# Attention bias loaded as one 1 MB transfer per block of four heads, and masked two heads at a time, on one Trainium2 core

## The chip, the cores and the metric

The kernel runs on 1 core of a Trainium2 chip, as one program. The metric is the time of one execution on the device in microseconds (us); lower is better. Engines are named as in the profile: PE is the matrix engine, DVE the vector engine, ACT the scalar engine, POOL the GpSimd engine, SP the engine that only issues transfers here.

## What is computed

Two layers on x of shape (8, 512, 512), float32. The first is a feed-forward layer (or, by a condition per sample, a small 4-wire circuit), then a layer norm. The second is a transformer layer with 16 heads of 32 columns, modulated by a time step embedding. Its attention reads a bias of 8 x 16 x 512 x 512 float32, 128 MB in all, and a mask of 8 x 1 x 512 x 512 bytes:

```
q, k, v = x @ Wq + bq, x @ Wk + bk, x @ Wv + bv            # 16 heads of 32
scores = einsum('bhqd,bhkd->bhqk', q / sqrt(32), k) + attention_bias
scores = where(src_mask, -inf, scores)
probs = softmax(scores)
ctx = einsum('bhqk,bhkd->bhqd', probs, v)
x = x + ctx @ Wo + bo
x = x + gelu2(layernorm(x) * g2 + beta2 @ W1 + b1) @ W2 + b2   # the feed-forward part, in words
```

## The kernel before

Three stages follow one another, with a barrier between them: `ffn_stage` (first layer), `attention_stage`, and `ffn_stage` again. Only the attention stage is touched.

**Work units.** A sample b (8 of them, `each_pair` unrolls odd and even ones) has 16 blocks m. A block is a group of four heads (`m // 4`) and 128 queries (`m % 4`); each of its four heads is one unit j: a 128x512 tile of scores. Blocks are counted 0 to 127 over all samples below where the text gives a global number.

**Order of the work.** Each engine has a list of its own, written out by hand, and they meet through semaphores. For block m, PE makes the scores of block m+1 (line 1247), the product with v of block m-1 (line 1264, the context), then four times: turns unit j of block m (line 1276, four 128x128 transposes of the exponentials into PSUM) and does three or so matmuls of another product beside it (line 1197). DVE adds scores and bias and finds the row's top in one instruction (line 1100, which waits for `masked` and `score_mm`), copies the turned units 1 and 3 out of PSUM (line 1107), and ACT takes the exponential (line 982) and copies the units 0 and 2 (line 989). PE's context of block m waits for those copies (`pt_even`, `pt_odd`), and PE's turn of unit j+2 waits for the copy of unit j.

Once per four blocks DVE has more to do. In a block with m % 4 == 3 it takes the reciprocals (line 1115); in one with m % 4 == 0 it normalises the group before (line 1120, `normalize`) and writes the low half of the context (line 1124, `context_lo`, which reads `at_normal` and `at_cth`, both in SBUF) between its scores of unit 3 and its copy of unit 3. In blocks 11 to 14 of a sample it also turns one quarter of the next sample's byte mask into bfloat16 after the copy of unit 3 (line 1079, `set_mask`). After blocks 8 and 9 PE turns the next sample's x (line 1204, `turn_x`), which waits for both copies.

**The bias.** `bias` holds 16 tiles of 128x512 (four blocks). SP loads two heads at a time (line 906, 512 KB), into the slots of block m as soon as PE has turned the first two, and then the last two, units of block m: these are the data of block m+4. POOL adds the mask, one head per instruction (line 951, bias += mask, in place), and counts `masked`; `set_mask` waits for that count before it overwrites a quarter of the mask. After the masks of block 13 POOL adds the output bias to the residual (line 955, four instructions). SP also issues, between the bias loads, the next x (line 917, at m = 0), the next mask (line 920, m = 1), the store of x2 (line 923, m = 4) and the residual (line 927, m = 8).

## Time and profile before

| | us |
|---|---|
| median of 3 runs | 2644.94 (2638.65 to 2649.93) |
| the profiled execution's own time | 2651.21 |
| its span | 2649.4 |
| PE busy over the span | 2447.0 (92%) |
| DVE busy | 1404.1 (53%) |
| ACT busy | 993.1 (37%) |
| POOL busy | 979.5 (37%) |
| attention stage, scores of the first block to the end of the last | about 893 to 1875 |

The profile is of one execution. Busy time is summed per engine; PE counts the matrix engine's pipelined matmuls, so its 92% is not 92% of its peak. The idle time of an engine is put down to whatever released it, from the semaphore events. DMA columns give the busy share of the 16 transfer engines: about half in the attention stage.

### The profile page before, as it was taken

Reading aid. Unit: us, or ns where it says so; the run is one execution under the profiler, and the core shown is the slowest. Engines: PE = TensorE matmul, PEld = TensorE weight load, DVE = VectorE, ACT = ScalarE, POOL = GpSimd, SP = SyncE. Lnnn points to the kernel's source line nnn. Section 1 sums busy time; section 2 is a strip of 40 time slices with the busy share of each in tenths; the row PEclk is TensorE's granted clock in tenths of the full one; section 3 lists DMA queues with packets and bytes.
Section 4 is the critical chain, followed back from the end, with each engine's and each line's share of the span. In section 5 each row is a group of like instructions: output and inputs, shape, how many; then the busy total and the mean of one; then the engine's idle time right before and its main releaser. Section 6 shows DMA issues by size and latency. Waiting matters only on the chain. (4 is left out here: it accounts for less than half of the span.)

```text
span 2649.4 us, 44273 instructions
## 1 busy us (share of the span) xinstructions
PE 2447.0 (92%) x16100; PEld 1920.0 (72%) x16100; DVE 1404.1 (53%) x2668; ACT 993.1 (37%) x1977; POOL 979.5 (37%) x806
## 2 busy tenths in 40 slices
PE   5999999999995789898989999998489999999999
PEld 4687787787783567676766667676378888888887
DVE  5354454454454677777677777777453333333322
ACT  4232231232230566666566656566231212111211
POOL 0031332332240565656565657666020122012200
PEclk9999999999997899999999999999789999999999
DMA  5201110110111555454555555545331001100100
GB/s 161 72 33 40 40 38 33 40 53 18 40 40 55 195 158 174 153 179 153 165 166 181 152 164 168 161 144 165 92 111 48 32 16 47 47 23 25 47 32 16
DMA packets 133361, 243.69 MB, mean 92 GB/s; under 512 B 13212, under 2 KB 17452, under 8 KB 133184
## 3 DMA queue, kind: packets, MB, share of 16 engines
q1 hardware_dynamic: 133184, 241.39, 28.4%
q8 instruction: 103, 1.69, 0.3%
q14 instruction: 74, 0.61, 0.1%
HBM read 216.17 MB, written 25.20 MB: 91 GB/s over the span
## 5 line engine op out<-in xcount | busy, mean ns | idle before, releaser
L951 POOL TENSOR_TENSOR at_bias<-at_bias,at_mask 128x512 f32<-128x512 f32 x512 | 587.3, 1173 | 381.0 <-DMA at_bias<-in_fside_Bx16xSxS 343.3
L648 DVE CAST L_hh<-L_hid 128x512 fp32r<-128x512 f32 x256 | 122.5, 478 | 797.9 <-PE L_acc L746 758.4
L487 ACT ACTIVATE L_hid<-L_turn,L_b1c 128x512 f32<-128x512 f32 x256 | 176.5, 690 | 983.9 <-PE L_turn L285 978.8
L283 PE MATMUL L_turn<-L_xth,L_w1h 128*128 128x512 f32 x1024 | 406.7, 397 | 7.7 <-ACT L_hid L487 5.4
L744 PE MATMUL L_acc<-L_w2h,L_hh 128*128 128x512 f32 x1024 | 403.1, 394 | 8.6 <-DVE L_hl L650 8.6
L284 PE MATMUL L_turn<-L_xth,L_w1l 128*128 128x512 f32 x1024 | 400.7, 391 | 0.0
L285 PE MATMUL L_turn<-L_xtl,L_w1h 128*128 128x512 f32 x1024 | 400.2, 391 | 0.0
L746 PE MATMUL L_acc<-L_w2l,L_hh 128*128 128x512 f32 x1024 | 400.1, 391 | 0.0
L745 PE MATMUL L_acc<-L_w2h,L_hl 128*128 128x512 f32 x1024 | 400.0, 391 | 0.0
L982 ACT ACTIVATE at_bias<-at_bias,at_neg_top 128x512 f32<-128x512 f32 x512 | 363.5, 714 | 44.3 <-DVE at_neg_top L1100 44.1
L1100 DVE CUSTOM_DVE_ANT_0 at_bias<-at_score,at_bias 128x512 f32<-128x512 f32 x512 | 333.0, 684 | 55.9 <-issue 29.8
L1276 PE MATMUL at_turn<-ident,at_bias 128*128 128x128 f32 x2048 | 314.7, 280 | 47.6 <-DVE at_pt L1107 33.7
L1276 PEld LDWEIGHTS at_turn<-ident,at_bias 128*128 128x128 f32 x2048 | 241.1, 142 | 131.1 <-issue 78.0
L989 ACT ACTIVATE at_pt<-at_turn 128x512 f32<-128x512 f32 x256 | 152.8, 597 | 285.4 <-PE at_turn L1276 285.3
L283 PEld LDWEIGHTS L_turn<-L_xth,L_w1h 128*128 128x128 f32 x1024 | 193.5, 189 | 74.5 <-issue 31.6
L650 DVE TENSOR_TENSOR L_hl<-L_hid,L_hh 128x512 fp32r<-128x512 f32 x256 | 231.8, 905 | 8.8
L744 PEld LDWEIGHTS L_acc<-L_w2h,L_hh 128*128 128x128 f32 x1024 | 193.2, 189 | 49.5 <-DVE L_hl L650 6.1
L1107 DVE COPY at_pt<-at_turn 128x512 f32<-128x512 f32 x256 | 174.2, 681 | 98.1 <-PE at_turn L1276 98.0
L285 PEld LDWEIGHTS L_turn<-L_xtl,L_w1h 128*128 128x128 f32 x1024 | 193.3, 189 | 41.3
L746 PEld LDWEIGHTS L_acc<-L_w2l,L_hh 128*128 128x128 f32 x1024 | 193.1, 189 | 40.6
L745 PEld LDWEIGHTS L_acc<-L_w2h,L_hl 128*128 128x128 f32 x1024 | 193.4, 189 | 39.3
L284 PEld LDWEIGHTS L_turn<-L_xth,L_w1l 128*128 128x128 f32 x1024 | 193.6, 189 | 38.7
(201 smaller groups left out, 3116.0 us busy)
## 6 DMA issues: line engine op xcount, KB each, us to landing
at_bias<-in_fside_Bx16xSxS SPq DMA_DIRECT2D x256, 512.0 KB, 3.7
L_xin<-in_x SPq DMA_DIRECT2D x8, 1024.0 KB, 5.4
L_xres<-in_x SPq DMA_DIRECT2D x8, 1024.0 KB, 5.4
at_xin<-x_scratch SPq DMA_DIRECT2D x8, 1024.0 KB, 6.5
at_xres<-x_scratch SPq DMA_DIRECT2D x8, 1024.0 KB, 6.9
L_xin<-x_scratch SPq DMA_DIRECT2D x8, 1024.0 KB, 5.5
L_xres<-x_scratch SPq DMA_DIRECT2D x8, 1024.0 KB, 5.5
x_scratch<-L_xres SPq DMA_DIRECT2D x7, 1024.0 KB, 4.3
```

What stands on the lines that cost most here:

```text
L283: nc_mm = pe.matmul(out, ah, bh, start=i == 0, stop=False)
L284: nc_mm = pe.matmul(out, al, bh, start=False, stop=False)
L285: nc_mm = pe.matmul(out, ah, bl, start=False, stop=i == n - 1)
L487: nc.scalar.activation(hid[m % 2][:, :], turn[m % 2][:, :], func, bias=b1c[:, m:m + 1]).then_inc(h_act, 1)
L650: nc.vector.tensor_tensor(hl[m % 2][:, :], hid[m % 2][:, :], hh[m % 2][:, :].bitcast(F32), ALU.subtract)\
L744: pe.matmul(acc[i][:, :], hh[m % 2][:, cut], w2h[:, m, :], start=m == 0, stop=False)
L745: pe.matmul(acc[i][:, :], hl[m % 2][:, cut], w2h[:, m, :], start=False, stop=False)
L746: mm = pe.matmul(acc[i][:, :], hh[m % 2][:, cut], w2l[:, m, :], start=False, stop=m == FT - 1)
L951: nc.gpsimd.tensor_tensor(tile, tile, mask[:, m % TT, :], ALU.add).then_inc(masked, 1)
L982: nc.scalar.activation(tile, tile, ACT.Exp, bias=neg_top[:, n % SLOTS:n % SLOTS + 1], scale=-1.0, accum_out=sums[:, n:n + 1]).then_inc(exp ...
L1100: nc.vector.tensor_tensor_reduce(bias[:, slot, :], score[j][:, :], bias[:, slot, :], -1.0, -MASKED, ALU.add, ALU.min, neg_top[:, slot:slot ...
L1276: mm = pe.transpose(turn[n % 2][:, k * P:(k + 1) * P], bias[:, n % SLOTS, k * P:(k + 1) * P], keep.ident[:, :])
```

## The change

Three things, all in the attention stage:

1. The bias of a block of four heads is one transfer of 1 MB in place of two of 512 KB, with one semaphore per ring position in place of two.
2. SP issues it when unit 3 of block m is turned. Before, the first half was issued when unit 1 was turned.
3. POOL's mask addition covers two heads (128x1024, the mask read twice by a zero stride) in one instruction, which adds 2 to `masked`.

```
-        bias_in = [[sem(f"bias_in{r}{i}") for i in range(2)] for r in range(4)]
+        bias_in = [sem(f"bias_in{r}") for r in range(4)]
...
-            def load_bias(b, m, i):
+            def load_bias(b, m):
                 tile, u = divmod(m, TT)
-                h = GROUP * tile + 2 * i
-                src = t["fside_Bx16xSxS_0"][b, h:h + 2, u * P:(u + 1) * P, :].rearrange("h p n -> p h n")
-                sp.dma_start(bias[:, m % 4 * 4 + 2 * i:m % 4 * 4 + 2 * i + 2, :], src).then_inc(bias_in[m % 4][i], 16)
+                src = t["fside_Bx16xSxS_0"][b, GROUP * tile:GROUP * tile + GROUP, u * P:(u + 1) * P, :].rearrange("h p n -> p h n")
+                sp.dma_start(bias[:, m % 4 * 4:m % 4 * 4 + 4, :], src).then_inc(bias_in[m % 4], 16)
...
-                        for i in range(2):
-                            wait_apart(sp, passed_sp, (turned, b * UNITS + GROUP * m + 2 * i + 2))
-                            load_bias(b + (m + 4) // BLOCKS, (m + 4) % BLOCKS, i)
+                        wait_apart(sp, passed_sp, (turned, b * UNITS + GROUP * m + GROUP))
+                        load_bias(b + (m + 4) // BLOCKS, (m + 4) % BLOCKS)
...
-                    for j in range(GROUP):
-                        if j % 2 == 0:
-                            pool.wait_ge(bias_in[m % 4][j // 2], b * 64 + 16 * (m // 4 + 1))
-                        tile = bias[:, m % 4 * 4 + j, :]
-                        nc.gpsimd.tensor_tensor(tile, tile, mask[:, m % TT, :], ALU.add).then_inc(masked, 1)
+                    pool.wait_ge(bias_in[m % 4], b * 64 + 16 * (m // 4 + 1))
+                    for i in range(GROUP // 2):
+                        tiles = bias[:, m % 4 * 4 + 2 * i:m % 4 * 4 + 2 * i + 2, :]
+                        nc.gpsimd.tensor_tensor(tiles, tiles, mask[:, m % TT:m % TT + 1, :].to_broadcast([P, 2, S]), ALU.add)\
+                            .then_inc(masked, 2)
```

The order of instructions on PE, DVE and ACT is the same as before. On SP it changes as follows, here around block 8 of a sample, where the residual is loaded. `at_turned` is PE's count of turned units; a register instruction stands before each wait. Before:

```order
L906 ISA [waits at_turned]
L906 DMA at_bias<-in_fside_Bx16xSxS 128x2x512
L71 REGISTER_ALU
L906 ISA [waits at_turned]
L906 DMA at_bias<-in_fside_Bx16xSxS 128x2x512
L71 REGISTER_ALU
L927 ISA [waits at_stored]
L927 DMA at_xres<-x_scratch 128x4x512
L71 REGISTER_ALU
L906 ISA [waits at_turned]
L906 DMA at_bias<-in_fside_Bx16xSxS 128x2x512
```

and now:

```order
L905 ISA [waits at_turned]
L905 DMA at_bias<-in_fside_Bx16xSxS 128x4x512
L71 REGISTER_ALU
L925 ISA [waits at_stored]
L925 DMA at_xres<-x_scratch 128x4x512
L71 REGISTER_ALU
L905 ISA [waits at_turned]
L905 DMA at_bias<-in_fside_Bx16xSxS 128x4x512
```

One wait and one transfer of four heads stand where two of each stood; the residual's load keeps its place between blocks.

On POOL, the masks of block 13 of a sample, the four additions to the residual and the masks of block 14. `at_bias_in..` is the semaphore of a bias load. Before:

```order
L951 TENSOR_TENSOR at_bias<-at_bias,at_mask 128x512 [waits at_bias_in10]
L951 TENSOR_TENSOR at_bias<-at_bias,at_mask 128x512
L951 TENSOR_TENSOR at_bias<-at_bias,at_mask 128x512 [waits at_bias_in11]
L951 TENSOR_TENSOR at_bias<-at_bias,at_mask 128x512
L955 TENSOR_TENSOR at_xres<-at_xres,at_bor 128x512 [waits at_xres_in]
L955 TENSOR_TENSOR at_xres<-at_xres,at_bor 128x512 x3
L951 TENSOR_TENSOR at_bias<-at_bias,at_mask 128x512 [waits at_bias_in20]
```

and now:

```order
L947 TENSOR_TENSOR at_bias<-at_bias,at_mask 128x1024 [waits at_bias_in1]
L947 TENSOR_TENSOR at_bias<-at_bias,at_mask 128x1024
L952 TENSOR_TENSOR at_xres<-at_xres,at_bor 128x512 [waits at_xres_in]
L952 TENSOR_TENSOR at_xres<-at_xres,at_bor 128x512 x3
L947 TENSOR_TENSOR at_bias<-at_bias,at_mask 128x1024 [waits at_bias_in2]
L947 TENSOR_TENSOR at_bias<-at_bias,at_mask 128x1024
```

A block has one wait and two instructions of 128x1024 where it had two waits and four instructions of 128x512; there is no wait between the two any more.

## Rows read from the trace of the kernel before

**Rows 1.** Windows view, the attention stage: stretch; us; busy of PE, PEld, DVE, ACT, POOL; PEclk; DMA; GB/s
```profile
900.00:1875.00 975.00, 886.88 (x9302) 673.63 (x9301) 719.28 (x1510) 608.53 (x1449) 606.60 (x529) 0.96 0.51 160
```

**Rows 2.** Waits view, 1000 to 1850: us in total, times, longest us
```profile
POOL at_bias L951 <- DMA at_bias<-in_fside_Bx16xSxS: 309.8, 159, 6.4
...
PE at_turn L1276 <- DVE at_pt L1107: 26.8, 28, 2.4
...
PE at_turn L1204 <- DVE at_pt L1107: 18.9, 12, 2.0
...
DVE at_bias L1100 <- POOL at_bias L951: 3.3, 7, 0.8
```

**Rows 3.** Groups of instructions on POOL, 860 to 1900
```profile
L951 POOL TENSOR_TENSOR at_bias<-at_bias,at_mask 128x512 f32<-128x512 f32 x512 | 587.3, 1173 | 381.0 <-DMA at_bias<-in_fside_Bx16xSxS 343.3 <-DVE at_mask L1079 36.1
L955 POOL TENSOR_TENSOR at_xres<-at_xres,at_bor 128x512 f32<-128x512 f32 x32 | 40.1, 1289 | 0.0
```

**Rows 4.** DMA view: issues, KB each, median us from issue to landing
```profile
at_bias<-in_fside_Bx16xSxS SPq DMA_DIRECT2D x256, 512.0 KB, 3.7
L_xin<-in_x SPq DMA_DIRECT2D x8, 1024.0 KB, 5.4
...
at_xres<-x_scratch SPq DMA_DIRECT2D x8, 1024.0 KB, 6.9
```

**Rows 5.** Timeline, block 124: its first mask, and DVE's first use of it
```profile
1826.86 1.16 POOL L951 TENSOR_TENSOR at_bias<-at_bias,at_mask 128x512 f32<-128x512 f32 x1 [3.06 <-DMA at_bias<-in_fside_Bx16xSxS]
...
1835.85 0.69 DVE L1100 CUSTOM_DVE_ANT_0 at_bias<-at_score,at_bias 128x512 f32<-128x512 f32 x1 [0.65 <-issue]
```

**Rows 6.** DVE lines by themselves: count, min/median/max ns, first and last start
```profile
L650 DVE TENSOR_TENSOR L_hl<-L_hid,L_hh x256: 691/693/1677, 33.5 to 2639.3; 128x512 fp32r<-128x512 f32 x128
...
L1079 DVE TENSOR_SCALAR at_mask<-at_mask x32: 414/417/1527, 879.3 to 1748.4; 128x512 bf16<-128x512 uint8 x32
...
L1124 DVE SCALAR_TENSOR_TENSOR at_ctl<-at_normal,at_bvc,at_cth x32: 744/748/3078, 928.7 to 1873.8; 128x512 fp32r<-128x512 f32 x32
```

**Rows 7.** Timeline, 1848 to 1852: POOL's masks of block 127 and DVE beside them
```profile
1849.19 2.29 POOL L951 TENSOR_TENSOR at_bias<-at_bias,at_mask 128x512 f32<-128x512 f32 x2
...
1848.95 3.08 DVE L1124 SCALAR_TENSOR_TENSOR at_ctl<-at_normal,at_bvc,at_cth 128x512 fp32r<-128x512 f32 x1 [0.30 <-ACT at_cth L1001]
```

**Rows 8.** Timeline of SP: issues of a block's second half
```profile
1134.31 0.37 SPq L906 DMA_DIRECT2D at_bias<-in_fside_Bx16xSxS  x1
...
1196.17 0.37 SPq L906 DMA_DIRECT2D at_bias<-in_fside_Bx16xSxS  x1
...
1212.92 0.37 SPq L906 DMA_DIRECT2D at_bias<-in_fside_Bx16xSxS  x1
...
1229.35 0.38 SPq L906 DMA_DIRECT2D at_bias<-in_fside_Bx16xSxS  x1
```

**Rows 9.** Timeline of DVE in blocks 32, 40, 43 and 44
```profile
1140.74 0.75 DVE L1124 SCALAR_TENSOR_TENSOR at_ctl<-at_normal,at_bvc,at_cth 128x512 fp32r<-128x512 f32 x1
...
1202.69 0.75 DVE L1124 SCALAR_TENSOR_TENSOR at_ctl<-at_normal,at_bvc,at_cth 128x512 fp32r<-128x512 f32 x1
...
1230.04 0.61 DVE L1079 TENSOR_SCALAR at_mask<-at_mask 128x512 bf16<-128x512 uint8 x1
1231.55 0.75 DVE L1088 SCALAR_TENSOR_TENSOR at_nat<-at_gen,at_bqc,at_nat 128x512 fp32r<-128x512 f32 x1 [0.91 <-ACT at_nat L972]
...
1235.85 0.75 DVE L1124 SCALAR_TENSOR_TENSOR at_ctl<-at_normal,at_bvc,at_cth 128x512 fp32r<-128x512 f32 x1
1236.52 0.68 DVE L1107 COPY at_pt<-at_turn 128x512 f32<-128x512 f32 x1
```

**Rows 10.** Timeline of PE: after block 40, and the context of block 44
```profile
1204.30 1.96 PE L1204 MATMUL at_turn<-ident,at_xin 128*128 128x128 f32 x8 [1.96 <-DVE at_pt L1107]
...
1237.61 0.64 PE L1264 MATMUL at_ctx<-at_pt,at_v 128*32 128x128 f32 x16
```

**Rows 11.** Timeline of POOL: the last two masks of block 43
```profile
1199.63 2.27 POOL L951 TENSOR_TENSOR at_bias<-at_bias,at_mask 128x512 f32<-128x512 f32 x2 [1.51 <-DMA at_bias<-in_fside_Bx16xSxS]
```

More of the change, by code:

```diff
@@ L899, in _ @@
             sp.dma_start(mask8[:, :, :], rows(t["mask_Bx1xSxS_bk0"][0, 0])).then_inc(mask_in, 16)
-            def load_bias(b, m, i):
+            def load_bias(b, m):
                 tile, u = divmod(m, TT)
-                h = GROUP * tile + 2 * i
-                src = t["fside_Bx16xSxS_0"][b, h:h + 2, u * P:(u + 1) * P, :].rearrange("h p n -> p h n")
-                sp.dma_start(bias[:, m % 4 * 4 + 2 * i:m % 4 * 4 + 2 * i + 2, :], src).then_inc(bias_in[m % 4][i], 16)
+                src = t["fside_Bx16xSxS_0"][b, GROUP * tile:GROUP * tile + GROUP, u * P:(u + 1) * P, :].rearrange("h p n -> p h n")
+                sp.dma_start(bias[:, m % 4 * 4:m % 4 * 4 + 4, :], src).then_inc(bias_in[m % 4], 16)
             for m in range(4):
                 sp.wait_ge(w_lo, m + 1)
-                for i in range(2):
-                    load_bias(0, m, i)
+                load_bias(0, m)
             def body(b, odd, first, last):
@@ L928, in body @@
                     if m + 4 < BLOCKS or not last:
-                        for i in range(2):
-                            wait_apart(sp, passed_sp, (turned, b * UNITS + GROUP * m + 2 * i + 2))
-                            load_bias(b + (m + 4) // BLOCKS, (m + 4) % BLOCKS, i)
+                        wait_apart(sp, passed_sp, (turned, b * UNITS + GROUP * m + GROUP))
+                        load_bias(b + (m + 4) // BLOCKS, (m + 4) % BLOCKS)
             each_pair(sp, body)
```

## Prediction

> **What bounds the kernel now.** I read the stretch of the attention stage first, then its waits, then the timeline around the few instructions in which DVE and POOL meet. The stretch says that PE bounds the stage: 887 of 975 us busy, DVE 719, POOL 607, the transfer engines 51% [rows 1]. The waits say who holds PE in what is left: mostly DVE's copy of a turned unit (line 1107), 26.8 us in front of the next turn and 18.9 us in front of the turn of x [rows 2]. POOL's idle time is nearly all waiting for the bias, 309.8 us, and DVE waits for POOL for 3.3 us in all [rows 2]. So the masks are made well ahead. The tightest place is in the last sample: block 124's first mask starts at 1826.86 and DVE takes that tile at 1835.85, 9.0 us later [rows 5]; in the other 127 blocks that lead is longer.
>
> **The change, part by part.** I sum against the profiled execution (span 2649.4, own time 2651.2) and add the sum to the median, 2644.9, which lies 6 us below it.
>
> *Fewer transfers.* 128 issues of 0.37 us [rows 8] leave SP, on which nothing waits but transfers; the bytes and the 2 KB pieces are the same. 0 us, hidden behind the 9 us lead above.
>
> *Later masks.* A block's first two heads are now asked for with the last two, 2.3 to 3.8 us later, and 1 MB lands 5.4 us after its issue when it is alone on the queue, against 3.7 for 512 KB; behind other traffic it took 6.9 [rows 4]. The first `masked` count comes after two heads, not one, 1.1 us more. Together 2.3 to 3.8, plus 1.7 to 3.2, plus 1.1: 5.1 to 8.1 us of a lead that is 9.0 less the first mask's 1.16 at the tightest place, 7.8 us. That takes both of the longest values at once, and there the issue is the short one; it holds: 0 us. Were the lead gone, DVE's line 1100 would wait, and ACT's exponential and PE's turn behind it.
>
> *Two heads per instruction.* One head takes 1.17 us, of which the trace does not show a fixed part; the pair now takes 2.27 [rows 3, 11]. The bounds for one instruction of 128x1024 are 1.2 us (all of it fixed) and 2.6 (twice line 955's 1289 ns). I take 2.25, what a pair takes, since the instruction still handles 1024 elements. POOL is idle 38% of the stage, so its own time is worth 0 us either way. What matters is what it blocks.
>
> *POOL and DVE in each other's way.* This is the term on which I forecast. Some DVE instructions take far longer than their median beside a POOL instruction: line 650, with both inputs in SBUF, 693 ns mostly but up to 1677; line 1079 417 and up to 1527; line 1124, again two SBUF inputs, 748 in 31 of 32 cases and 3078 once [rows 6]. The extra 984 and 1110 ns fit in the rest of one POOL instruction. In the one long case of line 1124, POOL ran masks without a gap: DVE asked at 1848.95, POOL went from one instruction to the next at 1849.19, and once more before its pair ended at 1851.48, and DVE was done at 1852.03, so that it got in only at about 1851.3 [rows 7]. The Trainium skill (SBUF — State Buffer, "Who interferes with whom") says it in the same way: the read and write ports shared by the two are an exclusive lock, a DVE instruction with two SBUF inputs needs it against a POOL instruction that reads SBUF, and the second to start blocks until the first has finished. The trace agrees for lines 650 and 1079 (one instruction's rest), and not in rows 7, where DVE was passed over twice. By the page the sum below is the forecast's, by rows 7 the first rival's.
>
> Before, line 1124 nearly always falls into a gap of POOL. In block 40 the last masks of block 43 run from 1199.63 to 1201.90 [rows 11] and line 1124 starts at 1202.69 [rows 9]. Now the masks of block 43 start when a transfer issued at 1196.17 [rows 8] has landed, 1196.17 + 5.4 = 1201.6, and run to 1203.8 and 1206.1. Line 1124 asks in the middle of the first. With the lock passed on at the next end it waits 1.1 us. PE is already waiting 1.96 us for DVE's very next instruction, the copy, in front of the turn of x [rows 10], so all of it reaches PE: 1.1 us in each of the 7 samples that turn an x, 8 us.
>
> Block 32 (block 0 of a sample): 1134.31 + 5.4 = 1139.7, first mask to 1142.0, line 1124 at 1140.74 [rows 8, 9]: it waits 1.2 us. Here PE has room: in block 44, built alike, the copy ends at 1237.20 [rows 9] and PE's context starts at 1237.61 [rows 10], 0.4 us. 0.8 us x 7 = 5 us. In block 4 of a sample line 1124 comes later against its load and meets the second instruction's end, 0.6 us against 0.4: 1 us over the run.
>
> Block 12 of a sample is the worst, because line 1079 comes in front of it. POOL's masks of block 45, asked for at 1212.92 [rows 8], run 1218.3 to 1222.8, line 955 four times to 1227.9, and then the masks of block 46, 1227.9, 1230.1, 1232.4. Line 1079 starts at 1230.04 [rows 9], at the boundary; if it just misses it, it waits 2.2 us. DVE has 0.91 us of idle time behind it [rows 9] and is then busy without a gap, so line 1124 asks 1.3 us later, at 1237.1. The masks of block 47, asked for at 1229.35 [rows 8], run 1234.8, 1237.0, 1239.3: the wait is 2.1 us. DVE's copy is 3.4 us late, PE 3.0. 3.0 x 7 = 21 us. If line 1079 slips in at the boundary, line 1124 waits 1.1 and this is 0.7 x 7 = 5 us. The other calls of line 1079 wait 0.4 to 1 us in front of gaps of DVE that cover it: 0.
>
> Sum: 8 + 5 + 1 + 21 = 35 us, and PE, which bounds the stage, has nothing with which to make it good. 2644.9 + 35 = **2680 us**, 1.3% slower. What a measurement of this kernel can tell from no change is about 0.5%, 13 us.
>
> **The rivals.**
>
> *The lock is held to the end of POOL's run.* Rows 7 speak for it, and line 1124 is the very instruction; the 56 long cases of line 650 speak against, none over one instruction. There is no wait between a block's two instructions now, so a run is 4.5 us. Blocks 8: to 1206.1, 3.4 x 7 = 24; block 0: 3.0 x 7 = 21; block 12: 21; 1 more: 67 us, 2712.
>
> *No meeting, so not slower.* The margin is small: line 1124 asks 6.5 us after the issue. If 1 MB of bias lands after 6.5 us or more, as the residual's does with its 6.9 [rows 4], line 1124 of blocks 0, 8 and 12 gets in before POOL starts and POOL waits instead, which costs nothing. Much the same follows if the two-head instruction takes not 2.25 but the 1.2 us of its lower bound, since line 1124 would then ask 0.1 us before the first one's end. Then only a few waits of line 1079 are left, 0 to 8 us: 2645 to 2653, taken as 2648. Against it: the 5.4 us of a lone 1 MB load.
>
> *Faster.* All the waiting at the shared ports that the stage has now is 2.3 us at line 1124 and some 4 us at line 1079. If short instructions removed it, and the change had no meeting elsewhere, 2638. That is still within what can't be told from no change. More would need PE to wait less for copies, and nothing in the change shortens DVE's own chain.
>
> *The lead is used up.* If each 1 MB took 6.9 us behind the residual and the sample's last blocks lost their lead, line 1100 would wait in the last sample, some 1 us in four blocks: 2649. It is small and adds to any case.
>
> **How the numbers follow.** The forecast, meeting with the lock passed on at an instruction's end: 0.42, its own range 19 us (line 1079 slips in) to 45 us (a two-head instruction of 2.6 us). Held to the run's end: 0.22. No meeting, or the lead alone: 0.32. Faster or the remainder: 0.04. 0.03 of the forecast's chance lies within 13 us of before. So faster 0.03, within 0.5% 0.35, slower 0.62. The range must reach to both neighbours: from 2643 to 2713.
>
> **What would show it.** In the profile after, line 1124 should have a median of about 1.8 us in place of 0.75, and longest values near 2.9; under the rival near 4.1. Line 1079 should be long in block 11 only. The wait of PE's turn of x for line 1107 should grow from 18.9 us by about 8, and waits of the context (line 1264) for line 1107 should appear. POOL's instruction should be 2.25 us, and the load land 5.4 us after its issue. The prediction is wrong if line 1124 stays at 0.75 us, or if DVE waits for POOL at line 1100 for more than a few us.

## The result, and the profile after

The changed kernel takes 2656.64 us, median of 6 runs (2654.53 to 2659.48), beside 2646.16 for the kernel before on the same chip: a ratio of 1.0043 with an interval of 1.0026 to 1.0059, 10.5 us slower. The forecast was 35 us slower, 1.3%. The direction came out, at less than a third of its size, and inside the half per cent of "no change" but for the interval's upper end. The two profiled executions that are read below took 2657.24 and 2651.21 us, so they differ by 6.0 us and not by 10.5.

I read the views of after in the order of [rows 1 to 6]. First the windows view of the attention stage (columns as in [rows 1]):

```profile
900.00:1875.00 975.00, 885.21 (x9263) 671.73 (x9262) 746.74 (x1507) 607.12 (x1449) 578.73 (x281) 0.96 0.47 160
```

DVE is busy 27 us longer with the same work, 746.7 against 719.3 [rows 1]. POOL is busy 28 us less, with half as many instructions. The waits view, 1000 to 1850:

```profile
POOL at_bias L947 <- DMA at_bias<-in_fside_Bx16xSxS: 345.9, 103, 8.4
...
PE at_turn L1273 <- DVE at_pt L1104: 29.1, 28, 2.4
...
PE at_turn L1201 <- DVE at_pt L1104: 21.0, 12, 2.5
```

PE's turn of x waits 2.1 us more for DVE's copy than in [rows 2], where the forecast wanted 8, and the turn of a unit 2.3 us more. The 3.3 us that DVE's scores waited for POOL are gone from the view. The masks, their load, and the two DVE lines that meet them (groups of POOL, DMA view, and the lines by themselves):

```profile
L947 POOL TENSOR_TENSOR at_bias<-at_bias,at_mask 128x1024 f32<-128x1024 f32 x256 | 558.0, 2202 | 418.5 <-DMA at_bias<-in_fside_Bx16xSxS 382.3
```

```profile
at_bias<-in_fside_Bx16xSxS SPq DMA_DIRECT2D x128, 1024.0 KB, 5.0
```

```profile
L1121 DVE SCALAR_TENSOR_TENSOR at_ctl<-at_normal,at_bvc,at_cth x32: 744/1099/1953, 927.0 to 1879.7; 128x512 fp32r<-128x512 f32 x32
...
L1076 DVE TENSOR_SCALAR at_mask<-at_mask x32: 416/1442/2398, 880.6 to 1754.2; 128x512 bf16<-128x512 uint8 x32
```

So the meeting takes place. (In these lines the three numbers behind the count are the shortest, the median and the longest duration in ns.) The median of `context_lo` (line 1121, 1124 before) grew from 748 to 1099 ns, not to the 1800 forecast. `set_mask` (line 1076, 1079 before) grew from 417 to 1442. Above those old medians, the 32 calls of `context_lo` wait 10.6 us in sum (2.3 before), and the 28 of `set_mask` that lie inside the samples 24.3 (2.2 before): 30 us of new waiting, for an end that is 10.5 us later.

**Block 40, the place of the forecast's first term.** Timeline of SP, POOL, DVE and PE:

```profile
1195.12 0.37 SPq L905 DMA_DIRECT2D at_bias<-in_fside_Bx16xSxS  x1
...
1199.93 2.13 POOL L947 TENSOR_TENSOR at_bias<-at_bias,at_mask 128x1024 f32<-128x1024 f32 x1 [2.17 <-DMA at_bias<-in_fside_Bx16xSxS]
...
1202.03 2.57 POOL L947 TENSOR_TENSOR at_bias<-at_bias,at_mask 128x1024 f32<-128x1024 f32 x1
...
1201.64 0.98 DVE L1121 SCALAR_TENSOR_TENSOR at_ctl<-at_normal,at_bvc,at_cth 128x512 fp32r<-128x512 f32 x1
...
1203.47 1.97 PE L1201 MATMUL at_turn<-ident,at_xin 128*128 128x128 f32 x8 [2.18 <-DVE at_pt L1104]
```

DVE asks 6.5 us after the issue, as forecast. But the load was there after 4.8 us (1199.93 - 1195.12), not 5.4; POOL's first instruction took 2.13, not 2.25; and DVE was done at 1202.62, so that it was in at about 1202.62 - 0.75 = 1201.87 if it then took the 0.75 us that it takes alone, 0.19 before the end that the trace gives for POOL's first instruction, 1202.06. Together 0.9 us, so the wait is 0.23 us and not 1.1. All of it reaches PE, whose wait is 2.18 where it was 1.96 [rows 10]. The mechanism is the one forecast, and its place on the clock was missed by less than a microsecond.

**Block 44, the place of the 21 us.** Timeline of DVE and POOL:

```profile
1228.07 2.13 POOL L947 TENSOR_TENSOR at_bias<-at_bias,at_mask 128x1024 f32<-128x1024 f32 x1
...
1228.90 1.59 DVE L1076 TENSOR_SCALAR at_mask<-at_mask 128x512 bf16<-128x512 uint8 x1
1230.41 0.75 DVE L1085 SCALAR_TENSOR_TENSOR at_nat<-at_gen,at_bqc,at_nat 128x512 fp32r<-128x512 f32 x1
...
1233.32 2.16 POOL L947 TENSOR_TENSOR at_bias<-at_bias,at_mask 128x1024 f32<-128x1024 f32 x1 [3.12 <-DMA at_bias<-in_fside_Bx16xSxS]
...
1234.72 1.30 DVE L1121 SCALAR_TENSOR_TENSOR at_ctl<-at_normal,at_bvc,at_cth 128x512 fp32r<-128x512 f32 x1
```

`set_mask` came 0.83 us after a boundary of POOL's run, not just behind it, and waited 1.17 us. The next DVE instruction, which had 0.91 us of idle time in front of it [rows 9], now has none. The whole trace stands 1.1 us earlier than that of before here, and 1234.72 is 1.13 earlier than the 1235.85 of [rows 9]: `context_lo` asks no later than it did. It waits 0.55 us, of which PE's slack of 0.4 takes most.

**The start of sample 3 (samples counted from 0), which the forecast did not name.** Timeline of DVE and PE, then the windows view around it (columns as in [rows 1], the last but two the granted clock):

```profile
1248.99 2.40 DVE L1076 TENSOR_SCALAR at_mask<-at_mask 128x512 bf16<-128x512 uint8 x1
...
1252.53 3.34 DVE L1112 RECIPROCAL at_normal<-at_sums 128x512 f32<-128x512 f32 x1
...
1256.56 0.77 PE L1273 MATMUL at_turn<-ident,at_bias 128*128 128x128 f32 x4 [2.08 <-DVE at_pt L1104]
1256.98 0.78 PE L1194 MATMUL at_gen<-at_wvh,at_xth 128*128 128x512 f32 x1
```

```profile
1256.50:1258.30 1.80, 1.74 (x7) 1.49 (x8) 1.73 (x5) 1.25 (x3) 1.37 (x1) 0.61 0.11 18
1258.30:1261.70 3.40, 1.20 (x9) 0.69 (x7) 0.00 (x0) 0.39 (x3) 0.00 (x0) 0.50 0.83 275
1261.70:1264.00 2.30, 2.30 (x28) 1.52 (x32) 0.53 (x1) 0.96 (x2) 0.18 (x1) 0.50 1.00 344
1264.00:1268.00 4.00, 4.00 (x37) 3.20 (x30) 1.51 (x6) 1.65 (x4) 4.00 (x2) 0.61 0.29 105
```

The same place in the trace of before, PE's timeline and the windows:

```profile
1256.27 0.63 PE L1276 MATMUL at_turn<-ident,at_bias 128*128 128x128 f32 x4 [0.90 <-DVE at_pt L1107]
1256.65 0.48 PE L1197 MATMUL at_gen<-at_wvh,at_xth 128*128 128x512 f32 x1
```

```profile
1256.20:1258.30 2.10, 1.76 (x11) 1.37 (x11) 1.74 (x5) 1.52 (x4) 0.61 (x1) 1.00 0.28 80
...
1261.70:1264.00 2.30, 2.30 (x37) 1.91 (x29) 1.91 (x5) 0.93 (x2) 1.76 (x2) 0.52 0.13 29
1264.00:1268.00 4.00, 4.00 (x24) 3.34 (x23) 2.06 (x7) 3.56 (x8) 0.00 (x0) 0.85 0.77 289
```

This `set_mask` asked at 1248.99, just behind a boundary of POOL's run, and waited 1.98 us, the "just misses" of the forecast, in another block. Behind it stands DVE's long reciprocal, so the copy behind that is late and PE idles 2.08 us in place of 0.90: 1.2 of the 1.98 us reach PE, 0.8 are covered. Right behind that idle time the granted clock is at 0.61 and 0.50 (the level of 1.2 GHz), where in the trace of before it is still at 1.00, and a matmul of 512 columns takes 0.78 in place of 0.48 us. The clock falls here in before too, but later and for less time: 5 us on, behind 2.60 us in which PE waits for nothing that the profile shows ("issue"). The last two lines of each window view show it, 0.52 and 0.85 against 0.50 and 0.61 at the same times in after. The period that ends with the first turn of sample 3 is 2.8 us longer than before, that of sample 5, built alike, 2.4. Not all of this can be put down to `set_mask`: at these two places every trace has that second idle time of PE, from 2.0 to 3.9 us, and in e3 and e8 below, where no `set_mask` waits there, the same periods come out up to 1.5 and 2.4 us longer than in before. A clean case is the start of sample 1 in a second trace of the changed kernel (e11): `set_mask` waits 1.93 us, PE idles 2.03 in place of 0.90, its clock is at 0.50 from 1013.0 to 1016.4, and the period is 10.80 in place of 8.10 us. Of these 2.7 us, 1.1 are idle time and the rest comes with the clock.

Over the stage the two traces differ as follows. A period is the time from one block's first turn of a unit to the next block's; each figure is the sum over the samples of what the changed kernel's period is longer, for the period that ends with the block named, in us. The second pair are two further traces of the same two kernels (e11 and e12, profiled executions of 2656.24 and 2644.83 us), and e7 is an experiment below.

| period ending with | first pair | second pair | e7 against before |
|---|---|---|---|
| block 0 (start of a sample) | +5.2 | +3.3 | +3.3 |
| block 1 | +0.2 | +0.4 | +2.6 |
| block 5 | +0.3 | 0.0 | +3.2 |
| blocks 9 and 10 | +3.7 | +5.3 | +7.8 |
| blocks 13 and 14 | -1.9 | +4.0 | +6.7 |
| others | -0.2 | -2.2 | -0.1 |
| block 4 of the first sample to block 127 | +7.3 | +10.8 | +23.6 |

The -1.9 is the last sample's: the 3.08 us of line 1124 in [rows 7] lies there in before, whose period is 2.6 us longer than that of after. Without the last sample blocks 13 and 14 give +1.1 us in the first pair and +1.2 in the second. The last sample also adds 2.0 to the +3.7 of blocks 9 and 10, with PE at the lower clock there in after alone and no x to turn.

**Block 8 at the same clock.** Blocks 9 and 10 swing most from pair to pair because of the clock. In block 8 PE's idle time in front of the turn of x is 1.96 us in six of the seven samples that turn one, in before as in e12, and around it the granted clock falls, not always and not for equally long. Windows of PE alone, block 8 of samples 5, 1 and 2 in e12, which is the kernel before, then of sample 2 in before and in after (us; busy of PE; PEclk; DMA; GB/s):

```profile
1571.91:1580.25 8.34, 5.31 (x72) 1.00 0.75 265
1074.34:1084.21 9.87, 6.84 (x72) 0.83 0.67 220
1195.92:1206.67 10.75, 7.72 (x72) 0.70 0.58 198
```

```profile
1198.88:1209.64 10.76, 7.73 (x73) 0.73 0.58 199
```

```profile
1197.84:1208.81 10.97, 7.72 (x73) 0.70 0.69 242
```

The same block of the same kernel takes 8.34, 9.87 or 10.75 us with the mean clock at 1.00, 0.83 or 0.70. In before and in after the clock was at the lower level for equally long in all seven samples, so these two can be compared: after's period is longer by 0.38, 0.43, 0.22, 0.25, 0.35, 0.53 and 0.29 us, and its `context_lo` waits 0.37, 0.44, 0.23, 0.27, 0.34, 0.54 and 0.28. The wait reaches the end whole, 2.5 us over the run. In e8, where `context_lo` does not wait, the six samples with the same clock agree with before within 0.01 us.

Could the clock be the cause of the 10.5 us? Over the executions on record the mean granted clock is 0.969 in the changed kernel and 0.969 in the kernel before. Among the 69 executions of the kernel before whose clock is on record, the time falls as the clock rises (correlation -0.82, 1.7 us for each 0.001). By that slope, the difference between the two kernels' clocks, 0.0005, is worth an estimated 0.8 us. So the clock blurs the single traces, and it is not what makes the loss.

### The profile page after: what moved, and what is told of

It is laid out like the page before. It is cut to its first block and busy times, and to the rows that moved or that the text cites. A ratio compares the mean times of both kernels' runs of the same rounds, so it can differ in the third digit from the quotient of the medians.

```text
span 2655.4 us, 43580 instructions
## 1 busy us (share of the span) xinstructions
PE 2450.7 (92%) x16100; PEld 1922.3 (72%) x16100; DVE 1435.3 (54%) x2668; ACT 992.4 (37%) x1977; POOL 950.0 (36%) x550
## 5 line engine op out<-in xcount | busy, mean ns | idle before, releaser
L947 POOL TENSOR_TENSOR at_bias<-at_bias,at_mask 128x1024 f32<-128x1024 f32 x256 | 558.0, 2202 | 418.5 <-DMA at_bias<-in_fside_Bx16xSxS 382.3
```

The lines of the kernel that those rows point to most:

```text
L947: nc.gpsimd.tensor_tensor(tiles, tiles, mask[:, m % TT:m % TT + 1, :].to_broadcast([P, 2, S]), ALU.add)\
```

## The experiments

The theories that the runs were to tell apart: that the *place* of the masks makes the cost, because of the moment of the load (the forecast's, with its size corrected); that the *length* of POOL's instruction does, or the 1 MB *transfer*, or the lost *lead*. Ratios are against the kernel before (2646.6 to 2647.4 us in these sessions), with their intervals.

### One half of the change at a time

e1 keeps the 1 MB load and masks one head at a time:

```
-                    for i in range(GROUP // 2):
-                        tiles = bias[:, m % 4 * 4 + 2 * i:m % 4 * 4 + 2 * i + 2, :]
...
+                    for j in range(GROUP):
+                        tile = bias[:, m % 4 * 4 + j, :]
+                        nc.gpsimd.tensor_tensor(tile, tile, mask[:, m % TT, :], ALU.add).then_inc(masked, 1)
```

> The changed kernel with one mask instruction per head (1.17 us each) in place of one per two heads; the 1 MB load, begun when the whole block is turned, stays. Ports theory (the cost is DVE waiting for POOL at the shared ports, and it comes from the masks' later place, not from the length of an instruction): masks start 5.0 us after the issue, so that DVE's context_lo, 6.5 us after it, still meets a run of masks; its median is 1.1 to 1.8 us against 0.75 before, set_mask is long too but by at most 1.2 us a time; the time is 3 to 9 us above before. Length theory (only the two-head instruction makes waits that reach PE): same as before within 3 us. Transfer theory (the cost is the load itself): the whole 10 us stay.

e2 keeps the loads of before and masks two heads at a time, each pair behind its own wait:

```
+                    for i in range(GROUP // 2):
+                        pool.wait_ge(bias_in[m % 4][i], b * 64 + 16 * (m // 4 + 1))
+                        tiles = bias[:, m % 4 * 4 + 2 * i:m % 4 * 4 + 2 * i + 2, :]
+                        nc.gpsimd.tensor_tensor(tiles, tiles, mask[:, m % TT:m % TT + 1, :].to_broadcast([P, 2, S]), ALU.add)\
+                            .then_inc(masked, 2)
```

> The kernel before with only the masks changed: two heads in one instruction, each pair after its own 512 KB load. Ports theory: POOL's runs stand where they stood, context_lo still falls into gaps and stays at 0.75 us; set_mask of block 11 of a sample waits up to 2.1 us in place of 1.1, which DVE's idle time covers: 0 to 3 us above before. Length theory: most of the 10 us. Transfer theory: no difference from before.

Measured: e1 2658.06 us, 1.0038 (1.0024 to 1.0053), all of the loss; e2 2645.24 us, 0.9991 (0.9981 to 1.0001), none. The two lines by themselves, in e1:

```profile
L1120 DVE SCALAR_TENSOR_TENSOR at_ctl<-at_normal,at_bvc,at_cth x32: 745/1051/4103, 929.0 to 1879.4; 128x512 fp32r<-128x512 f32 x32
...
L1075 DVE TENSOR_SCALAR at_mask<-at_mask x32: 416/778/2053, 879.7 to 1752.9; 128x512 bf16<-128x512 uint8 x32
```

and in e2:

```profile
L1124 DVE SCALAR_TENSOR_TENSOR at_ctl<-at_normal,at_bvc,at_cth x32: 740/747/1334, 930.2 to 1865.9; 128x512 fp32r<-128x512 f32 x32
...
L1079 DVE TENSOR_SCALAR at_mask<-at_mask x32: 409/416/2361, 880.8 to 1743.6; 128x512 bf16<-128x512 uint8 x32
```

With the load late and the instructions short, `context_lo` waits as in after. With the instructions long and the load early it is at 747 ns. The two-head instruction makes `set_mask` wait in block 11 of every sample, to 1.3 to 1.7 us (8.0 us in sum; the 2361 ns are of a call ahead of the first sample), in front of DVE's 0.91 us of idle time, and the kernel is no slower for it. The length theory falls, and with it goes the forecast's fear of line 1079 in block 11. e1 by itself fits the transfer theory as well as the place theory, since all of the loss stays (the place theory had 3 to 9 us, and 10.1 came); the next pair parts them. And the loss does not follow the sum of the waits: `set_mask` waits 11.7 us inside the samples of e1 against 24.3 in after, for the same loss.

### Masks that hardly read

e3 (the changed kernel) and e4 (the kernel before) add the mask to 2 of the 512 columns; POOL keeps its place, its waits and its counts:

```
-                        tiles = bias[:, m % 4 * 4 + 2 * i:m % 4 * 4 + 2 * i + 2, :]
+                        tiles = bias[:, m % 4 * 4 + 2 * i:m % 4 * 4 + 2 * i + 2, 0:2]
```

> The changed kernel with the mask added to 2 of the 512 columns of each head only (the rest of the mask is left out), so that POOL's instructions are very short and hold no port. To be read against the kernel before with the same cut. Ports theory: context_lo at 0.75 and set_mask at 0.42 us throughout, and the two cut kernels are equal within 3 us. Transfer theory: this one is still 7 to 10 us slower than the cut kernel before.

> The kernel before with the mask added to 2 of 512 columns only (the rest of the mask is left out). Both theories: 0 to 5 us under the kernel before, the most that the few port waits and the waits for set_mask are worth there.

Measured: e3 2644.88 us, 0.9991 (0.9982 to 1.0000); e4 2644.40 us, 0.9995 (0.9983 to 1.0007). With POOL nearly idle the changed load costs nothing, with the same 1 MB transfers at the same moments. The transfer theory falls. A lack of lead would vanish too where the masks take no time, so the lead is left to e8. The line of `context_lo` in e3 has no wait left (maximum 753 ns, 1953 in after):

```profile
L1121 DVE SCALAR_TENSOR_TENSOR at_ctl<-at_normal,at_bvc,at_cth x32: 745/748/753, 929.1 to 1869.7; 128x512 fp32r<-128x512 f32 x32
```

e4 shows what the meetings of the kernel before are worth: 1.3 us by its ratio, 4.5 at most, and its interval allows none.

### The masks moved by a microsecond

e7 is the changed kernel with two POOL additions of 160 columns on a tile of their own ahead of each block's masks, 456 ns each, so that the masks begin 0.9 us later:

```
+                    for i in range(2):
+                        nc.gpsimd.tensor_tensor(spare[:, :], bor[:, 0:160], bor[:, 0:160], ALU.add).then_inc(spared, 1)
+                        pool.wait_ge(spared, b * 2 * BLOCKS + 2 * m + i + 1)
```

> The changed kernel with two short POOL additions on a spare tile (160 columns each, chained by a semaphore) ahead of each block's masks, so that a run of masks starts some 0.9 us later after its load. Sizes theory (the prediction's mechanism holds and only the point at which context_lo meets the masks was off: 0.3 us of the first instruction were left, not 1.1): context_lo is now 1.9 to 2.2 us long in blocks 0, 8 and 12 of a sample, the block after 8 grows by another 0.7 to 0.9 us and those after 0 and 12 by 0.5 to 0.8; 10 to 20 us above the changed kernel, about 2670. Absorption theory (DVE's later work takes up any such wait): within 4 us of the changed kernel.

Measured: 2676.66 us, 1.0124 (1.0108 to 1.0141), 20 us above the changed kernel. The line of `context_lo`, and PE's wait in front of the turn of x, 900 to 1875 (20.1 us before, 22.2 after):

```profile
L1124 DVE SCALAR_TENSOR_TENSOR at_ctl<-at_normal,at_bvc,at_cth x32: 745/1986/2384, 930.4 to 1899.1; 128x512 fp32r<-128x512 f32 x32
```

```profile
PE at_turn L1204 <- DVE at_pt L1107: 28.6, 13, 3.6
```

The median wait is 1.24 us now, what the forecast had assumed for the change itself. The loss against before is 30 us by the medians, near the 35 of the forecast, and PE's turn of x waits 8.5 us longer, where it had said 8. The table above shows that the loss lies in the blocks it named, behind blocks 0, 4, 8 and 12, and at the sample starts, which it did not. So the term of block 8 was priced well, wait and way to the end, and only the moment of the meeting was not. The others were not: e7 gives 2.6 us at block 0 (forecast 5), 3.2 at block 4 (1), 6.7 at block 12, or 8.2 without the last sample (21), and 3.3 at the sample starts (0). That the sum comes near 35 is in part luck. The waits of `set_mask` are about as long in sum as in after (27.7 us inside the samples, 24.3 in after); what grew is the sum at `context_lo`, from 10.6 to 31.4.

### The masks moved out of the way

e8 is the changed kernel with POOL held, by semaphores that exist already, until DVE has copied unit 3 and has done the `set_mask` behind it. The masks come later than in the changed kernel, in DVE's other stretches; in block 8 of the first sample they begin 1.5 us after `context_lo` has asked, against 1.6 us before it in after:

```
-                        pool.wait_ge(mask_set, b * TT + m + 1)
+                        pool.wait_ge(mask_set, b * TT + min(m + 3, TT))
+                    elif m >= 14 and not last:
+                        pool.wait_ge(mask_set, b * TT + TT + m - 13)
+                    if not first or m >= 3:
+                        pool.wait_ge(pt_odd, b * (UNITS // 2) + 2 * m - 4)
```

> The changed kernel with POOL's masks of block m+3 held back until DVE has copied unit 3 of block m (behind context_lo) and, in the four blocks concerned, has done set_mask. So the masks are later still, but meet neither. Ports theory: context_lo at 0.75 us and set_mask at 0.42 us but for the odd case, the time is back at that of the kernel before, 2643 to 2650. Lead theory (the masks come too late): slower than the changed kernel, with DVE waiting for masked in front of its scores.

Measured: 2646.65 us, 1.0002 (0.9992 to 1.0013). Later masks, and all of the loss gone. The line of `context_lo`, and what POOL waits for, 900 to 1875:

```profile
L1125 DVE SCALAR_TENSOR_TENSOR at_ctl<-at_normal,at_bvc,at_cth x32: 744/747/752, 929.3 to 1870.8; 128x512 fp32r<-128x512 f32 x32
```

```profile
POOL at_bias L951 <- DVE at_pt L1108: 339.8, 95, 8.1
```

One meeting is left: `set_mask` of block 11 waits 0.92 us in each of the seven samples, for the last of the additions to the residual, and nothing comes of it. POOL has time for the holding back: its waits for the load have become waits for the copy. With the lead shorter than in the changed kernel and no loss, the lead theory falls; DVE's scores wait for POOL nowhere in this view. The loads are those of the changed kernel, the instructions too, and only the place of the masks differs: the place is the cause. How the 10.5 us divide between `context_lo` and `set_mask` no run shows by itself, since e8 moves the masks away from both.

### The moment of the load alone

e10 is the kernel before with nothing merged: both 512 KB loads of a block are issued when unit 3 is turned.

```
+                        wait_apart(sp, passed_sp, (turned, b * UNITS + GROUP * m + GROUP))
                         for i in range(2):
-                            wait_apart(sp, passed_sp, (turned, b * UNITS + GROUP * m + 2 * i + 2))
                             load_bias(b + (m + 4) // BLOCKS, (m + 4) % BLOCKS, i)
```

> The kernel before, with its two loads of 512 KB and one mask instruction per head, but both loads issued when unit 3 is turned. So the moment moves and nothing is merged. Place theory (what counts is where the run of four masks falls against DVE's context_lo, 6.5 us after the issue): the run is from about 3.5 to 8.1 us after the issue, context_lo meets its third instruction and waits 0.2 to 1.1 us, and the time is 5 to 20 us above before. If only the 1 MB transfer counts: same as before.

Measured: 2653.52 us, 1.0020 (1.0011 to 1.0028).

```profile
L1124 DVE SCALAR_TENSOR_TENSOR at_ctl<-at_normal,at_bvc,at_cth x32: 745/1009/4362, 929.9 to 1873.5; 128x512 fp32r<-128x512 f32 x32
```

The moment alone brings the same waits at `context_lo` (11.9 us in sum over all 32, as in e1, of which 3.6 and 3.4 are one call of the last sample) and nearly the same at `set_mask` (12.5 us inside the samples, 11.7 in e1), and a loss of 5.3 us, between 2.9 and 7.4. e1 lost 10.1 (6.4 to 14.0). The moment makes at least a good part of the loss. Where the other half is in e1 and after, the runs leave open: it is neither in the sums of these waits nor in the mean granted clock (0.969 in both), and the intervals of e1 and e10 overlap a little.

### The same two again

> The changed kernel once more, for a second trace. Ports theory: the same waits at context_lo (1.0 to 1.3 us in blocks 8, 12) and set_mask, 2653 to 2660. In the first trace 5.2 of 5.7 us lay at two places, the starts of samples 3 and 5, where a set_mask of block 14 had waited 2 us in front of the long reciprocal and PE ran at half clock for a while. If that is part of the mechanism, it is there again in samples where that set_mask is long; if it was chance, it is elsewhere or nowhere.

> The kernel before once more, for a second trace and as a control of the timing: 2640 to 2652, ratio 1 within 0.15%; context_lo at 0.75 us in all blocks but the odd one in the last sample.

Measured: e11 2657.42 us, 1.0047 (1.0034 to 1.0060); e12 2646.88 us, 1.0002 (0.9993 to 1.0012). The size of the loss repeats; its place does so only in part. In the second pair (table above) the sample starts give less, a late `set_mask` now in front of sample 1, and blocks 9 and 13 more. The traces of the unchanged kernel differ by 7.5 us over the stage between themselves (939.9 and 932.4, first turn of block 4 to that of block 127). Of these, 4.3 lie in the period that ends with block 9, where e12 was at the lower clock for less time, and 2.6 in that of block 13, which has the long call of [rows 7] in before alone: the longest `context_lo` of e12 is 0.95 us. So a difference of one pair of traces says little about a term of one or two microseconds, unless the clock is the same in both.

### A shorter reciprocal

I took DVE's reciprocal, 3.35 us in front of a copy that PE waits for, to be what makes late copies costly. It computes 512 columns of which 16 differ. e5 (changed kernel) and e6 (kernel before) take it of the 16 sums and spread it with a copy:

```
-                of = sums[:, phase * PHASE:(phase + 1) * PHASE].unsqueeze(2).to_broadcast([P, PHASE, HD])
-                nc.vector.reciprocal(spread, of).then_inc(inv_set, 1)
+                nc.vector.reciprocal(inv[:, :], sums[:, phase * PHASE:(phase + 1) * PHASE]).then_inc(inv_small, 1)
+                dve.wait_ge(inv_small, b * PHASES + phase + 1)
+                nc.vector.tensor_copy(spread, inv[:, :].unsqueeze(2).to_broadcast([P, PHASE, HD])).then_inc(inv_set, 1)
```

> The changed kernel with the reciprocals taken on 128x16 and spread to 128x512 by a copy, in place of one reciprocal of 128x512 (3.35 us): DVE is some 2.3 us shorter once per four blocks. PE waits about 34 us in 32 places for the copy behind that instruction; they should go: 20 to 35 us under the changed kernel. Against the same edit of the kernel before: slack theory (port waits cost time only where DVE is late already): equal within 4 us; if they cost wherever they fall: still some 10 us above it.

> The kernel before with the same short reciprocal and copy. 20 to 35 us under the kernel before, by the 34 us that PE waits behind the long reciprocal. If those waits only move to the next copy, less than 5.

Measured: e5 2616.33 us, 0.9897 (0.9881 to 0.9912); e6 **2598.98 us**, 0.9826 (0.9811 to 0.9842), the fastest version here, 47.6 us under the kernel before. Groups of DVE in before, the long one, and in e6:

```profile
L1115 DVE RECIPROCAL at_normal<-at_sums 128x512 f32<-128x512 f32 x32 | 107.1, 3348 | 1.0 <-ACT at_bias L982 1.0
```

```profile
L1117 DVE COPY at_normal<-at_inv 128x512 f32<-128x512 f32 x32 | 27.3, 853 | 1.1
...
L1115 DVE RECIPROCAL at_inv<-at_sums 128x16 f32<-128x16 f32 x32 | 7.9, 248 | 1.0 <-ACT at_bias L983 1.0
```

and PE's waits for the copies in e6, 900 to 1875 (the first was 20.1, the second 33.7 before):

```profile
PE at_turn L1206 <- DVE at_pt L1108: 20.1, 13, 2.0
...
PE at_turn L1278 <- DVE at_pt L1108: 3.8, 6, 0.6
```

DVE has 72 us less to do, and the 33.7 us that PE waited behind the reciprocal are nearly gone. The gain of 47.6 is more than those 30 and more than I expected. The mean granted clock of e6 is 0.973 against 0.969, by the slope given above an estimated 6 to 7 us; the remaining ten or so I did not separate. With this edit the change costs 17.4 us (2616.33 - 2598.98), not 10.5: with the reciprocal's wait gone the waits at the ports do not become cheap. The theory that they would be absorbed once DVE has slack is wrong. Nor is each of them dearer: there are more of them, probably since the shorter DVE work moves `context_lo` against the masks. Its waits sum to 17.5 us in e5 and 1.1 in e6, against 10.6 and 2.3 in after and before, and in block 4 of a sample it waits 0.95 to 1.29 us in six of the eight samples, where in after it waited in two. And some 5 of the 17.4 us go with the clock (0.970 in e5, 0.973 in e6; the same slope, an estimate). PE still waits 20.1 us for the copy behind `context_lo` in front of its turn of x in e6, and in e5 the periods that end with blocks 9 and 10 are 8.4 us longer in sum, more than any others; the median of block 9 over the samples that turn an x is 10.73 us in e5 and 9.68 in e6, in part by the clock again.

e9 puts the guard of e8 into e5:

> The changed kernel with both the short reciprocal and the masks held back behind DVE's copy and set_mask. Ports theory: the 17 us by which the changed kernel with the short reciprocal lies above the old one with the same edit (2616 against 2599) are all port waits, so holding the masks back gives them back: 2596 to 2604. If part of the 17 us comes from the load, 2605 or more.

Measured: 2605.66 us, 0.9848 (0.9835 to 0.9861). The guard gives back 10.7 of the 17.4 us, and the time misses the 2596 to 2604 expected if all 17.4 were port waits that it removes. The expectation laid 2605 or more to the load; of the 6.7 us that stay the timeline shows another source, in block 12 of each sample (POOL and DVE of e9):

```profile
1210.84 5.46 POOL L957 TENSOR_TENSOR at_xres<-at_xres,at_bor 128x512 f32<-128x512 f32 x4
...
1216.26 4.25 POOL L952 TENSOR_TENSOR at_bias<-at_bias,at_mask 128x1024 f32<-128x1024 f32 x2
...
1219.32 1.75 DVE L1127 SCALAR_TENSOR_TENSOR at_ctl<-at_normal,at_bvc,at_cth 128x512 fp32r<-128x512 f32 x1
```

The guard held the masks of block 13 back, the four additions to the residual come behind them, and the masks of block 14 are pushed into `context_lo`, which waits 1.0 us. The guard moved a meeting there instead of removing it, and the periods that end with block 13 are 5.0 us longer in sum than in e6. I did not run a guard for this one, so a share of the load in the rest is not excluded.

## Why the prediction came out as it did

**Fewer transfers, 0 us.** Right as far as the runs tell: e3, with 128 transfers of 1 MB, is at 0.9991.

**Later masks, 0 us of lead.** Right: DVE's scores do not wait for POOL in after, and e8 has later masks still and loses nothing.

**Two heads per instruction, 2.25 us.** The duration was near: 2.13 to 2.15 us where no DVE instruction comes between, and it costs nothing by itself (e2).

**POOL and DVE in each other's way, +35 us. This is the step that failed.** Its mechanism was right, the meeting of POOL's masks with DVE at the ports, passed on at an instruction's end; its size was wrong, above all in the terms of block 12 (21 forecast, 1.1 measured) and block 8 (8 forecast, 2.5 measured), and a term at the sample starts was put at nothing:

- *Block 8, 1.1 us x 7 = 8.* Measured 0.23 us in block 40 and 0.22 to 0.53 over the seven samples, 2.5 us together at the same clock. It rested on three figures that were all a little high: the load at 5.4 (4.8 there, median 5.0), the instruction at 2.25 (2.13), the ports passed on at the instruction's end (some 0.19 earlier). Each is off by 0.1 to 0.6 us; the term is a small difference of larger numbers and shrank to less than a third, in block 40 to a fifth. The 5.4 was taken from a 1 MB load of x in another stage [rows 4].
- *Block 12, 3.0 us x 7 = 21.* Measured +0.16 us a sample. It took a wait of 2.2 us for line 1079, where 1.2 was found, of which DVE's 0.91 us of idle time left next to nothing; and the second meeting of 2.1 us needed the first. The prediction had named the other case (line 1079 slipping in at the boundary, 5 us) and chose the dearer, with no row that spoke for it. This one choice was 16 of the 35 us. The measured case was neither of the two: line 1079 asked 0.83 us behind the boundary.
- *Blocks 0 and 4, 5 + 1.* Measured 0.2 and 0.3. The wait in block 0 is 0.33 to 0.47 us in five samples and none in two, PE's slack there 0.4.
- *Missing:* the `set_mask` of block 14 in front of the long reciprocal: 5.2 us in the first pair at two sample starts, where the size of each is uncertain, and 2.7 at the clean one in the second. The prediction put "the other calls of line 1079" at 0, covered by gaps of DVE. Of the wait of this call only 0.8 us are covered: 1.98 us made PE idle 1.2 us more, 1.93 us 1.1, and 1.10 us in e7 0.3, and behind the two long ones the clock fell as well.

**The rivals.** *Held to the end of POOL's run* (2712): no single wait in after is longer than one instruction (2.40 us with its own 0.42 in it). It is not dead all the same: three calls in other traces waited to the end of a run (last section). *No meeting* (2648): nearer by its time than the forecast (its own range ends at 2653, the forecast's begins at 2664), wrong by its mechanism, since the meetings are there and e3 or e8 take 10 us away with them. *Lead used up* (2649): did not happen. e7 shows that the forecast's mechanism gives nearly the forecast's time when the masks begin 0.9 us later, though with the terms divided otherwise; the measured case lay between the forecast and the rival, on a slope of some 20 us in 0.9 us. A range of cases was right here, and the chance should have been spread over that slope, not put on one end.

**What would show it.** Line 1124 at 1.8 us: 1.10. Line 1079 long in block 11 only: wrong, it is 1.76 us in block 12 as well, and long at times in blocks 13 and 14. The turn of x +8: +2.1. New waits of the context for the copy: none, there is one of 1.2 us in either trace.

## What to carry to other kernels

The loss came from the place of the masks on the clock, and e8 got it back without touching the loads. Moving a load moves the work that waits for it, and that work can meet another engine at a shared port though no wait in the program joins them; before merging transfers, look at what the consumer will then run beside, instruction by instruction. A cost that is the difference of several durations (landing, length, handover) should be given as a range over the slack beside it, since 0.9 us decided here between 10 and 30 us. Before two traces are compared block by block, look whether the granted clock is the same in both: here it alone moved a block from 8.3 to 10.8 us. And if an engine that waits for loads a third of its time can be held until the other one's critical instructions are through, the conflict costs nothing (e8), as long as the held work does not pile up on the next one (e9).

## What the runs showed of the hardware that I had not expected

- DVE gets the shared ports a little before the end that the trace gives for POOL's instruction, if its own work then takes what it takes alone. In block 40 it was in 0.19 us ahead, and the `set_mask` at 1248.99, done at 1251.39, was in at 1250.97, 0.13 us ahead of the end that the next line shows. Ends on POOL are rough in a profile, so this may lie in the records. The Trainium skill (SBUF — State Buffer, "Who interferes with whom") has the second to start blocked until the first has finished; the traces agree but for this last tenth, and for the calls passed over below.

```profile
1248.96 2.14 POOL L947 TENSOR_TENSOR at_bias<-at_bias,at_mask 128x1024 f32<-128x1024 f32 x1
```

- The reverse of it: `set_mask` asked 0.03 us after this instruction had begun and waited for nearly all of it. In block 14 of the first sample it asked 0.015 us before an instruction of POOL began, with no gap to the one ahead, and did not wait at all. A few hundredths of a microsecond decide over a whole instruction, so the same code gives 0.42 us in one sample and 2.40 in another.
- The POOL instruction behind the one that DVE waited for is longer in its turn: 2.57 to 2.62 us behind a `context_lo` that got in, against 2.13 to 2.15 (block 40: the second mask 2.57, the first 2.13), and about 2.33 behind the shorter `set_mask`.
- `context_lo` was passed over more than once in three traces of kernels with one-head masks, each time once and in block 12 of the last sample: 3.08 us in before [rows 7], 4.10 in e1, 4.36 in e10, against 0.75 alone. In all three it got in only when POOL's run of masks without a gap ended, as the first rival had it. In e12, a second trace of the kernel before, the same call did not wait, and in the kernels with two-head masks the longest was 2.51 (e11). Why, the runs don't say.
- One instruction of 128x1024 takes 2.13 to 2.15 us against 2.27 for the pair of 128x512 [rows 11]: little of POOL's time is per instruction. In e3 an instruction on 128x4 takes 0.20 us, which bounds that part.
